# Layers 3 and 4 of a coupling network on the two halves of TensorE's array, and a turned order of PSUM banks

## What is computed

```python
# attention: 16 heads of 8 features, on the left 128 features
att = softmax(einsum('nqhd,nkhd->nqkh', q, k) / scale, axis=2)
out = einsum('nqkh,nkhd->nqhd', att, v).reshape(N, S, E // 2) @ Wo.T + bo
# coupling: three cycles, token by token
def _coupling_net(h, w1, b1, w2, b2, w3, b3, w4, b4):
    h = _gelu(h @ w1 + b1)              # 256 -> 256
    h = _gelu(h @ w2 + b2)              # 256 -> 128
    h = _gelu(h @ w3 + b3)              # 128 -> 64
    return jax.nn.sigmoid(h @ w4 + b4)  # 64 -> 1
out = x
for _ in range(3):
    tf = _coupling_net(out, ...)
    coupling = 0.1 + adaptive_range * (0.7 * gf + 0.3 * tf - 0.5) * 2.0
    out = out + coupling * _twist(out)
```

## Time and profile before

| | |
|---|---|
| median of 3 runs | 3422.21 us (3420.38 to 3422.49) |
| span of the profiled execution, first to last instruction | 3418.2 us |
| runs' median less that span | 4.0 us |
| mean granted clock of TensorE, share of full | 0.986 |
| PE, DVE, ACT, POOL busy | 3280.1, 2961.0, 2896.0, 976.6 us |

### The profile page before, as it was taken

One profiled execution on the slowest core, in us unless ns is written; L12 is line 12 of the kernel. 1 busy time (PEld: TensorE's weight loads), 2 busy tenths in 40 slices (PEclk: granted clock), 3 DMA queues, 4 the chain that ended last, 5 costly groups with the idle time before them and its releaser, 6 DMA issues.

```text
span 3418.2 us, 55797 instructions
## 1 busy us (share of the span) xinstructions
PE 3280.1 (96%) x19328; PEld 931.1 (27%) x19328; DVE 2961.0 (87%) x5517; ACT 2896.0 (85%) x3806; POOL 976.6 (29%) x1382
## 2 busy tenths in 40 slices
PE   6989999999999999999999999999999999999987
PEld 2222232322323232232322323232232322323222
DVE  7999989888898988989888898988989888898942
ACT  3868979798897979889798897979989798896975
POOL 5012060421506033060421406033060421505024
PEclk7998999999999999999999999999999999999999
DMA  3111111121112111111121111111121121111001
GB/s 89 26 41 43 37 44 32 43 49 43 51 33 54 39 49 43 43 50 32 43 50 43 51 33 50 41 46 47 36 57 33 43 49 44 38 32 50 7 22 37
DMA packets 97337, 144.71 MB, mean 42 GB/s; under 512 B 49312, under 2 KB 59936, under 8 KB 89248
## 3 DMA queue, kind: packets, MB, share of 16 engines
q1 hardware_dynamic: 93360, 123.83, 13.7%
q0 software_dynamic: 3696, 17.31, 2.7%
HBM read 34.61 MB, written 32.51 MB: 20 GB/s over the span
## 4 chain that ended last, share of the span: by engine, by line
PE 69%; DVE 14%; ACT 8%; issue 4%; SPq 2%; POOL 2%; DMA 1%; DVEq 0%; POOLq 0%
PE heads_ps L503 24%; PE ring_ps L470 15%; PE scoresT_ps L488 11%; DVE max_parts L949 10%; PE scoresT_ps L590 7%; ACT p_sb L700 4%; PE scoresT_ps L595 3%; DVE stats L960 2%; PE scoresT_ps L598 2%; ACT headsT L709 1%; PE scoresT_ps L601 1%; PE ring_ps L532 1%; SPq L337 1%; PE scoresT_ps L518 1%; PE heads_ps L470 1%
## 5 line engine op out<-in xcount | busy, mean ns | idle before, releaser
L949 DVE TENSOR_REDUCE max_parts<-ring_ps 128x1 f32<-128x512 f32 x3741 | 2365.5, 682 | 230.0 <-PE ring_ps L470 171.1
L700 ACT ACTIVATE p_sb<-scoresT_ps 128x1024 f32<-128x1024 f32 x2048 | 1970.2, 1025 | 84.6 <-PE scoresT_ps L488 60.8
L470 PE MATMUL ring_ps<-k_rows,q_rows 48*128 48x512 bf16 x3741 | 1078.0, 385 | 23.5 <-DVE max_parts L949 14.4
L503 PE MATMUL heads_ps<-p_sb,v_sb 128*9 128x512 f32 x8192 | 1073.3, 596 | 17.9 <-ACT headsT L709 11.9
L488 PE MATMUL scoresT_ps<-q_rows,k_rows 51*128 51x512 bf16 x4096 | 1021.8, 384 | 15.0 <-ACT p_sb L700 7.5
L470 PEld LDWEIGHTS ring_ps<-k_rows,q_rows 48*128 48x128 bf16 x3741 | 263.5, 94 | 1319.9 <-DVE max_parts L949 1209.6
L1210 POOL CAST max_wide<-max_all 128x16 bf16<-128x16 f32 x128 | 25.1, 196 | 1753.7 <-DVE max_all L955 1753.7
L590 PE MATMUL scoresT_ps<-state,w 128*128 128x512 f32 x736 | 365.4, 619 | 5.9 <-DVE state L1013 3.9
L488 PEld LDWEIGHTS scoresT_ps<-q_rows,k_rows 51*128 51x128 bf16 x4096 | 207.7, 94 | 243.7 <-ACT p_sb L700 219.9
L811 ACT ACTIVATE p_sb<-scoresT_ps,b 128x512 f32<-128x512 f32 x180 | 123.5, 686 | 165.6 <-PE scoresT_ps L590 164.6
L503 PEld LDWEIGHTS heads_ps<-p_sb,v_sb 128*9 128x9 f32 x8192 | 124.7, 89 | 289.6 <-issue 278.6
(11 more groups left out here) (206 smaller groups left out, 2757.7 us busy)
## 6 DMA issues: line engine op xcount, KB each, us to landing
q_rows<-parts SPq DMA_DIRECT2D x744, 32.0 KB
k_rows<-parts SPq DMA_DIRECT2D x744, 32.0 KB
x_sb<-in_x SPq DMA_DIRECT2D x16, 1024.0 KB, 4.9
x_in<-in_x SPq DMA_DIRECT2D x15, 1024.0 KB, 5.1
out<-x_sb SPq DMA_DIRECT2D x15, 1024.0 KB, 3.9
out<-x_in POOLq DMA_DIRECT2D x15, 1024.0 KB, 7.8
q_rows<-max_rows SPq DMA_DIRECT2D x512, 3.0 KB
feat_h<-headsT SPq DMA_DIRECT2D x512, 16.0 KB
```

Of the source, the lines that this page charges most:

```text
L470: e.matmul(ring_bank(max_taken, u + 1), q_rows[rows, slot, pair, h * BANK + qb * P:h * BANK + (qb + 1) * P], k_rows[rows, slot, pair, kh * ...
L503: m = e.matmul(heads_ps[32 * j:32 * j + DH + 1, :], v_sb[:, b % 2, kb, 4 * (group % NG) + j, 0:DH + 1], p_sb[:, n % 2, j, :], start=(kb == ...
L700: e.activation(p_sb[:, n % 2, 2 * two:2 * two + 2, :].rearrange("p h n -> p (h n)"), scoresT_ps[:, 2 * two * BANK:(2 * two + 2) * BANK], A ...
L949: e.tensor_reduce(max_parts[:, gi % 2, kh, col:col + 1], bank_of(max_taken, u + 1), AX.X, ALU.max).then_inc(max_taken, 1)
```

## The change

In layer 3, each half's 512 tokens are taken as two groups of 256. Both groups have the same weights; the one goes through the array's columns 0 to 63 and the other through columns 64 to 127, so that their outputs stand in the partitions 0 to 63 and 64 to 127 of the first 256 places of one bank. One gelu takes all 128 partitions by 256. Layer 4 takes the two groups from there: one through the array's rows 0 to 63, one through rows 64 to 127, into two neighbouring banks. The tanh takes both banks in one instruction, and for batch 15, whose banks are not neighbours in one tensor, in two. `w4`, `b3` and `w4_all` stand twice, in both halves of the partitions, for which two more loads are issued.

Since layer 4 now takes two banks at once, the banks of a cycle are given by a table, `FIRST_BANK`, and `BANK_LEFT_BY` names the beat whose evacuation a beat waits for. The first pair of scores in a step now takes the banks 2 and 3 and the second one the banks 0 and 1, with the wait for `freed[RING]` moved to the first pair, and the ring gives out bank 3 no more in the last two beats of a stage.

```diff
 FFN_BANKS = 3
+HALF = BANK // 2
+
+
+FIRST_BANK = (2, 1, 0, 2, 1, 0, 1, 0, 2, 0)
+BANK_LEFT_BY = (8, 9, 9, 0, 1, 2, 4, 5, 6, 7)
...
-        b1, b2, b3 = sb("b1", [P, 2]), sb("b2", [P, 1]), sb("b3", [D // 2, 1])
+        b1, b2, b3 = sb("b1", [P, 2]), sb("b2", [P, 1]), sb("b3", [P, 1])
...
-        w4, g3 = sb("w4", [D // 2, 1]), sb("g3", [D // 2, 1])
-        w4_all, g3_all = sb("w4_all", [D // 2, P]), sb("g3_all", [D // 2, P])
+        w4, g3 = sb("w4", [P, 1]), sb("g3", [D // 2, 1])
+        w4_all, g3_all = sb("w4_all", [P, P]), sb("g3_all", [D // 2, P])
...
-        ones = sb("ones", [D // 2, P])
+        ones = sb("ones", [P, P])
...
-        def layer_bank(b, cycle, l):
-            i = (CYCLE * cycle + l) % FFN_BANKS
+        def layer_bank(b, l, second=0):
+            i = FIRST_BANK[l] + second
             return banks[RING - 1 + i] if b == N - 1 else scoresT_ps[:, i * BANK:(i + 1) * BANK]
+
+        def coupling_banks(l):
+            i = FIRST_BANK[l]
+            return scoresT_ps[:, i * BANK:(i + 2) * BANK].rearrange("p (s n) -> p s n", s=2)[:, :, 0:HALF]
...
-            load(w4[:, :], a["w4"])
+            for s in range(2):
+                load(w4[64 * s:64 * s + 64, :], a["w4"])
...
-            load(b3[:, :], a["b3"].rearrange("(p k) -> p k", k=1))
+            for s in range(2):
+                load(b3[64 * s:64 * s + 64, :], a["b3"].rearrange("(p k) -> p k", k=1))
...
-                if n == 0 and two == 1:
+                if n == 0 and two == 0:
                     e.wait_ge(*freed[RING])
                 if b or n:
                     e.wait_ge(exp_done, 2 * step_of(b, n) + two - 1)
                 for side in range(2):
                     rows = slice(64 * side, 64 * side + ROWS + MROWS)
-                    m = e.matmul(scoresT_ps[:, (2 * two + side) * BANK:(2 * two + side + 1) * BANK],
+                    m = e.matmul(scoresT_ps[:, (2 - 2 * two + side) * BANK:(3 - 2 * two + side) * BANK],
...
                 if CYCLE * cycle + l >= FFN_BANKS:
-                    e.wait_ge(hid_done[k], layer_end(before, cycle, l) - FFN_BANKS)
-                elif b == N - 1 and freed[RING - 1 + l]:
-                    e.wait_ge(*freed[RING - 1 + l])
+                    left_by = BANK_LEFT_BY[l]
+                    e.wait_ge(hid_done[k], layer_end(before, cycle - (1 if left_by > l else 0), left_by))
+                elif b == N - 1 and freed[RING - 1 + FIRST_BANK[l]]:
+                    e.wait_ge(*freed[RING - 1 + FIRST_BANK[l]])
...
                 if layer == 3:
                     e.wait_ge(hid_done[k], end_of(before, cycle, 2, c))
-                    o = e.matmul(ps[0:D // 2, :], w3[:, :], hidden[k][:, 1, c, :], start=True, stop=True)
+                    for s in range(2):
+                        o = e.matmul(ps[64 * s:64 * s + 64, 0:HALF], w3[:, :],
+                                     hidden[k][:, 1, c, s * HALF:(s + 1) * HALF], start=True, stop=True)
                 if layer == 4:
                     e.wait_ge(hid_done[k], end_of(before, cycle, 3, c))
-                    o = e.matmul(ps, w4_all[:, :], hidden[k][0:D // 2, 1, 2 + c, :], start=True, stop=True)
+                    for s in range(2):
+                        rows = slice(64 * s, 64 * s + 64)
+                        o = e.matmul(layer_bank(b, l, s)[:, 0:HALF], w4_all[rows, :],
+                                     hidden[k][rows, 1, 2 + c, 0:HALF], start=True, stop=True)
                 o.then_inc(ffn_done[k], 1)
...
                     cycle, beat = divmod(j, CYCLE)
+                    if j == BEATS - 2:
+                        turn[RING] = float("inf")
                     if valid(b - 1):
                         coupling(b - 1, cycle, beat)
                     if valid(b - 1) and cycle == 0:
@@ -698,7 +717,7 @@
...
                 e.activation(p_sb[:, n % 2, 2 * two:2 * two + 2, :].rearrange("p h n -> p (h n)"),
-                             scoresT_ps[:, 2 * two * BANK:(2 * two + 2) * BANK], ACT.Exp,
+                             scoresT_ps[:, (2 - 2 * two) * BANK:(4 - 2 * two) * BANK], ACT.Exp,
...
                 if layer == 3:
-                    e.activation(hidden[k][0:D // 2, 1, 2 + c, :], ps[0:D // 2, :], ACT.Gelu,
+                    e.activation(hidden[k][:, 1, 2 + c, 0:HALF], ps[:, 0:HALF], ACT.Gelu,
                                  bias=b3[:, 0:1]).then_inc(hid_done[k], 1)
...
-                    e.activation(couples[k][:, c, :], ps, ACT.Tanh, bias=b4_half[:, 0:1],
-                                 scale=0.5).then_inc(hid_done[k], 1)
+                    if b == N - 1:
+                        e.activation(couples[k][:, c, 0:HALF], layer_bank(b, l, 0)[:, 0:HALF], ACT.Tanh,
+                                     bias=b4_half[:, 0:1], scale=0.5)
+                        e.activation(couples[k][:, c, HALF:BANK], layer_bank(b, l, 1)[:, 0:HALF], ACT.Tanh,
+                                     bias=b4_half[:, 0:1], scale=0.5).then_inc(hid_done[k], 1)
+                    else:
+                        e.activation(couples[k][:, c, :].rearrange("p (s n) -> p s n", s=2), coupling_banks(l), ACT.Tanh,
+                                     bias=b4_half[:, 0:1], scale=0.5).then_inc(hid_done[k], 1)
                     if cycle < 2 or b == N - 1:
                         scale_coupling(b, cycle, l)
```

More of the change, by code:

```diff
@@ L577, in coupling @@
                 k, before = track(b)
-                ps = layer_bank(b, cycle, l)
+                ps = layer_bank(b, l)
                 if CYCLE * cycle + l >= FFN_BANKS:
-                    e.wait_ge(hid_done[k], layer_end(before, cycle, l) - FFN_BANKS)
-                elif b == N - 1 and freed[RING - 1 + l]:
-                    e.wait_ge(*freed[RING - 1 + l])
+                    left_by = BANK_LEFT_BY[l]
+                    e.wait_ge(hid_done[k], layer_end(before, cycle - (1 if left_by > l else 0), left_by))
+                elif b == N - 1 and freed[RING - 1 + FIRST_BANK[l]]:
+                    e.wait_ge(*freed[RING - 1 + FIRST_BANK[l]])
                 if layer == 1:
@@ L638, in tensor_program @@
                 project_v(0, h)
-            e.wait_ge(weights_loaded, 16 * 18)
+            e.wait_ge(weights_loaded, 16 * 20)
             done = 0
@@ L1144, in vector_program @@
                     e.wait_ge(const_dve, 1)
-                    e.wait_ge(weights_loaded, 16 * 18)
+                    e.wait_ge(weights_loaded, 16 * 20)
                     e.tensor_scalar(w4_all[:, :], ones[:, :], w4[:, 0:1], None, ALU.mult)
-                    e.tensor_scalar(g3_all[:, :], ones[:, :], g3[:, 0:1], None, ALU.mult)
+                    e.tensor_scalar(g3_all[:, :], ones[0:D // 2, :], g3[:, 0:1], None, ALU.mult)
                     e.tensor_scalar(b4_half[:, :], b4[:, :], 0.5, None, ALU.mult)
```

## The result

The changed kernel takes 3401.07 us in the median of 4 runs (3397.87 to 3406.32), beside 3421.30 for the kernel before on the same chip (3420.38 to 3422.49): a ratio of 0.9942, 95% interval 0.9928 to 0.9956. It is 20 us faster, where 30 were forecast. The profiled execution took 3397.87 us, its span is 3396.1.

A forecast was written before the change was run, and what follows sets the result against it. DVE was taken to bound each stage's middle third, PE most of the last. Twelve stages at 1.8 us and two at 1.2 (24.0), plus 5.9 in the ending, gave 29.9: 3422.2 becomes 3392 us, range 3370 to 3410.

The forecast's parts named there:

- Overlap of the halves: Layers 3 and 4 on PE: both column or row groups run together, saving 0.43 us per layer.
- half the overlap: Rival, 12 in 100: passes start in program order, each site saves 0.21 us, giving 3400 us.
- Gelu, tanh, banks, start: Layer 3's gelu 0.46 us; tanh unchanged except batch 15, about 0.17 more each; banks taken as 0; start nothing.
- The last third: Stage's third coupling cycle: beats 24 and 26 save 0.43 us each, beat 28's gelu starts 0.13 sooner and is 0.22 shorter.
- The first third: Stage's first coupling cycle: an earlier PE closes only the one hole in DVE's run, 0.59 us.
- Behind batch 14's attention: Coupling stage after that attention: DVE's hole there isn't PE's to close, so the gain is 1.2 us.
- Behind batch 1's: Coupling stage after batch 1's attention: DVE's hole there isn't PE's to close, so the gain is 1.2 us.
- The ending: Coupling of batches 14 and 15 after the last attention: 0.43 + 1.9 + 3.6 = 5.9 us saved.
- The wide rival: Rival "more of PE counts", 16 in 100: DVE's run begins earlier, up to 5.2 us a stage, 3344; likelier 3370.

The follow-up runs named there:

- last_cycle: Changed kernel with layers 3 and 4 divided only in the stages' third cycle and the ending, undivided in cycles one and two; 3398.26 us, 0.9936 of the kernel before.
- first_cycles: Changed kernel with layers 3 and 4 divided only in the stages' first two cycles and the ending, undivided in the third; 3415.87 us, 0.998 of the kernel before.
- y_first_after: Full change, plus ACT copying the output projection y of beats 5 and 6 ahead of the layer norm; 3389.63 us, 0.9905 of the kernel before.
- moved_units: y_first_after plus three max units per stage moved from the second cycle's beats to the third's; 3381.39 us, 0.9883 of the kernel before.
- spread_units: As moved_units, with the third cycle's 25 max units laid out more evenly over its beats; 3389.59 us, 0.9905 of the kernel before.
- ending_only: Changed kernel with layers 3 and 4 divided only for batches 14 and 15, coupled in the ending; 3419.53 us, 0.9995 of the kernel before.

## Why the prediction was right, and where it was off

The time lies in the range and the sign was right; the forecast of 3392 was 9 us low, and a third of the forecast gain didn't come. By its own steps:

*Overlap of the halves: right.* 0.43 us was forecast for each, 0.42 measured at both layers. By the Trainium skill, page "TensorE: Matmul & The Clock Gate", section on what overlaps, matmuls start strictly in program order. In the form in which the prediction applied this, with both passes of one half ahead of the other half's first, the trace doesn't bear it out: the starts of the halves stand together, and layer 3's pair took 0.58, not the 0.79 that this would make of it (0.58 and one more quarter pass of 0.21). The rule itself is not refuted: no record tells in which order the engine's list holds the four passes, and taken from the two halves by turns they would satisfy it. That the median of 3401 lies by the rival "half the overlap" (3400) is chance.

*Gelu, tanh, banks, start: right.* 0.47 us for 0.46; the banks by themselves 0.9999.

*The last third: the sum right but for 0.1, its terms less so.* 1.2 us were forecast, 1.10 measured (24.59 for 25.69). Layer 3 of beat 24 saved its 0.42, but a max unit behind it then waited for a bank of the ring that DVE frees (0.19 us in the chain), so layer 1 of beat 25 came only 0.24 sooner (62.31 for 62.55 behind the stage's start). Layer 4 of beat 26 counted in full: layer 2 of beat 27 came 0.66 sooner. The third gelu came 0.90 sooner, 0.24 more and not 0.13, and its shorter length gave the last 0.20. So an error of 0.19 was met by one of 0.11 the other way, which is luck. The gelu does start when the accumulator is read (1507.86), as the prediction said.

*The first third: here the prediction failed.* Its step "what an earlier PE closes is the one hole in DVE's run, 0.59 us" took the row's releaser, PE, for the cause. PE came earlier and then waited 1.27 us for a ring bank that DVE itself frees, behind y. What PE did take off the hole was 0.12 us, and none of it reached cycle 3. The step was 0.59 too high in each of twelve stages, 7.1 us. That POOL and ACT hold y, and that its time would not move, the prediction had right: the savings of PE turned into ACT's wait for POOL's offset, 0.15 us before and 0.59 after.

*Behind batch 14's attention: 1.2 forecast, 0.15 measured* (72.73 to 72.58, last exp to first exp). PE idled 1.46 us before L602, the granted clock over the next 3.8 us was 0.59, and L602's four matmuls took 3.47 us for 1.96. In last_cycle, without this fall, that stage took 71.72, 1.0 less than before. First_cycles and y_first_after, divided in the first cycles like the changed kernel, show two falls each in that stage, and last_cycle and the kernel before none; moved_units, divided too, shows none. The sum had no term for the clock. Behind batch 1's the gain was 1.39.

*The ending: 5.9 forecast, 5.5 measured* (134.5 to 129.0 behind the last exp). A new cycle waits for POOL as forecast. Timeline of POOL in the changed kernel:

```profile
3345.07 1.77 POOL L1302 TENSOR_TENSOR state<-state,k_rows 128x512 f32<-128x512 f32 x1
```

L1302 ends at 3346.84, L602 starts at 3346.94.

Added up, 12 stages at 1.11, 1.39, 0.15 and 5.5 are 20.4 us, beside 20.2 in the medians. The two profiled executions differ by 22.1, with stages and attentions up to 1.7 us longer here and there in either.

*The wide rival* ("more of PE counts") did not happen in this order of work, but its mechanism is real: once y's place in ACT's queue is changed and the units are moved, the early layers count, 21 us of them.

## What to carry to other kernels

What a profile names as ending an engine's idle time is the last link and need not be the cause: before a hole is counted as a gain, follow what the engine so named itself waits for, one step further, since a bank can lead back to the engine with the hole. When a shorter operation brings nothing, look for an in-order queue in which its consumer stands behind something slower, and try the reordering together with the change; here the reordering and the division of the first two cycles were each worth nothing alone and 11 us together. With the ending, the last cycle and the moved units it came to 41. Work moved into a stage's free time has to be checked at the seams as well: two layouts with equal stages were 8 us apart in the median.

## What the hardware showed that was not expected

TensorE's granted clock fell to one half for a few us behind short idle times of PE, and each fall that was priced cost 1.5 to 1.6 us: at 3116 in the changed kernel (1.46 us idle ahead of it, L602 1.51 us longer), and in eight attentions of spread_units (1.58 us each). The same idle time at another seam of that kernel was followed by none, so idleness goes before a fall but doesn't settle it. Nor do the profiled executions show that a kernel in which PE waits more meets more of them: between 300 and 3280 us there is one in the kernel before, two in the changed one, none in moved_units and nine in spread_units. They also blur medians: ending_only and first_cycles differ by 3.7 us with stages of 74.80 and 74.78 and endings of 129.3 and 128.8. A part of that is early in the program: in ending_only the clock stood at 0.50 from 257.5 to 298.5 us, in first_cycles at 0.79 in the mean.

Cutting an f32 matmul of 512 columns in two, with four weight loads for two, cost nothing measurable (1.01 us for 1.00).
